# Two causal score products of a gated linear attention as 64-row matmul pairs, each head parity in a PSUM bank of its own

## The reference

```python
def step1(hk, inp):
    qi, ki, si, gi = inp
    hk = hk * gi[:, :, None, :] + ki[..., None] * si[:, :, None, :]
    return (hk, jnp.einsum('bhk,bhkm->bhm', qi, hk))
_, ok = jax.lax.scan(step1, hk0, (q, k, s_norm, g))
qv = jax.nn.softmax(ok, -1)
def step2(hv, inp):
    qvi, si, vi, gi = inp
    hv = hv * gi[..., None] + si[..., None] * vi[:, :, None, :]
    return (hv, jnp.einsum('bhm,bhmv->bhv', qvi, hv))
_, ov = jax.lax.scan(step2, hv0, (qv, s_norm, v, g))
```

## Time and profile before

| | us |
|---|---|
| median of 3 runs | 1521.48 (1519.7 to 1524.4) |
| time of the profiled execution | 1518.72 |
| span of its trace | 1516.6 |

### The profile page before, as it was taken

The page is one execution under the profiler, slowest core; times in us unless marked ns, Lnnn a source line. Parts: engine busy times, 40 slices in busy tenths (PEclk is TensorE's granted clock), DMA queues, the critical chain, the costliest instruction groups (busy, mean ns, idle before and its releaser), DMA issues.

```text
span 1516.6 us, 31405 instructions
## 1 busy us (share of the span) xinstructions
PE 1456.9 (96%) x10520; PEld 1291.4 (85%) x10520; DVE 1217.1 (80%) x3006; ACT 961.4 (63%) x2531; POOL 828.6 (55%) x937
## 2 busy tenths in 40 slices
PE   5798999999999999999999999999999999999975
PEld 3577989889889988988989888889988989989764
DVE  3668888888888888888888888888888888888642
ACT  3456666766666667666666766666667666666541
POOL 2355555656665565565556656655565565556420
PEclk9999999999999999999999999999999999999987
DMA  8230100011110001111100011110001111000000
GB/s 250 98 100 18 24 10 23 17 24 24 25 24 15 18 16 24 24 24 24 24 10 23 17 24 24 24 24 10 23 16 24 24 24 24 21 13 18 17 7 14
DMA packets 113102, 45.03 MB, mean 30 GB/s; under 512 B 86192, under 2 KB 109104, under 8 KB 112944
## 3 DMA queue, kind: packets, MB, share of 16 engines
q1 hardware_dynamic: 112944, 43.03, 11.3%
HBM read 26.74 MB, written 16.25 MB: 28 GB/s over the span
## 4 chain that ended last, share of the span: by engine, by line
PE 91%; DVE 3%; issue 2%; POOL 1%; ACT 1%; DMA 1%; SPq 0%; POOLq 0%; DVEq 0%; ACTq 0%
PE bank L444 76%; PE bank L450 7%; PE bank L685 5%; PE bank L770 2%; PE bank L532 1%; DVE a_conv L887 1%; PE bank L738 0%; DVE a_rC L909 0%; ACT x_prob L1331 0%; SPq L433 0%; DMA x_prob<-in_ctxT 0%; DVE x_nmax L1013 0%; DMA x<-in_x 0%; PE bank L541 0%; DVE x L1035 0%
## 5 line engine op out<-in xcount | busy, mean ns | idle before, releaser
L1331 ACT ACTIVATE x_prob<-bank,x_nmax 128x77 f32<-128x77 f32 x1024 | 248.5, 329 | 51.2 <-DVE x_nmax L1013 50.2
L1013 DVE TENSOR_REDUCE x_nmax<-bank 128x4 f32<-128x308 f32 x256 | 120.1, 469 | 109.8 <-PE bank L444 106.0
L1344 ACT ACTIVATE x_probT<-bank 128x256 f32<-128x256 f32 (+1 forms) x256 | 112.2, 438 | 98.3 <-PE bank L685 98.1
L1497 POOL TENSOR_TENSOR a_orinv<-a_ove,mhalf 128x8 f32<-128x8 f32 x32 | 65.1, 2035 | 199.1 <-DVE a_ove L952 199.1
L444 PE MATMUL bank<-x_Vbd,x_probT 128*128 128x34 f32 (+1 forms) x1280 | 162.5, 267 | 0.7 <-DVE x_o L1027 0.7
L887 DVE SCALAR_TENSOR_TENSOR a_conv<-a_raw,cw,a_conv 128x256 f32<-128x256 f32 x384 | 155.0, 478 | 7.5 <-POOL a_conv L1459 7.5
L444 PEld LDWEIGHTS bank<-x_Vbd,x_probT 128*128 128x128 f32 x1280 | 158.0, 192 | 1.1 <-DVE x_o L1027 1.1
L685 PE MATMUL bank<-ident,x_prob 128*128 128x128 f32 x640 | 114.6, 277 | 0.4 <-ACT x_prob L1331 0.3
L909 DVE RECIPROCAL a_rC<-bank 128x512 f32<-128x512 f32 x32 | 107.1, 3348 | 0.6 <-PE bank L444 0.6
L912 DVE TENSOR_TENSOR a_AT<-bank,tri 128x512 f32<-128x512 f32 x128 | 87.7, 685 | 23.9 <-PE bank L444 23.9
L444 PE MATMUL bank<-x_K_bd,x_Q_stack 128*128 128x308 f32 x256 | 94.5, 369 | 8.6 <-ACT x_prob L1331 5.2
(11 more groups left out here) (271 smaller groups left out, 5264.0 us busy)
## 6 DMA issues: line engine op xcount, KB each, us to landing
x<-in_x SPq DMA_DIRECT2D x32, 256.0 KB, 2.6
out<-x SPq DMA_DIRECT2D x32, 256.0 KB, 2.2
x_K_stack<-k_hi SPq DMA_DIRECT2D x64, 77.0 KB, 2.6
k_hi<-f_sT_hi SPq DMA_DIRECT2D x5, 512.0 KB, 2.8
k_lo<-f_sT_lo SPq DMA_DIRECT2D x5, 512.0 KB, 3.8
v_tok<-x_probT SPq DMA_DIRECT2D x10, 256.0 KB, 3.4
x_KT_lo<-k_lo SPq DMA_DIRECT2D x32, 77.0 KB, 2.3
x_Vbd<-v_tok SPq DMA_DIRECT2D x128, 9.6 KB
```

The costliest lines, as they stand in the source:

```text
L1013: dve.tensor_reduce(nmax[:, u % 2, :], X0[:, 0:UH * S2].rearrange("p (h s) -> p h s", h=UH), AX.X, ALU.min).then_inc(on.x_max, 1)
L1331: ins = act.activation(prob[:, col:col + S2], X0[:, i * S2:(i + 1) * S2], ACT.Exp, scale=-1.0, bias=nmax[:, u % 2, i:i + 1])
L1344: act.activation(probT[:, g[0]:g[-1] + 1, :].rearrange("p h t -> p (h t)"), X1[:, 0:len(g) * P], ACT.Copy).then_inc(on.x_pT, 1)
```

## The change

Both triangular products are cut along the contraction into rows 0 to 63 and rows 64 to 127, which hold two heads each. The upper half (`i = 0`) writes A0 in `a_A` and A1 in `a_P`, the lower half the other bank. `a_q_bd` shrinks to two column blocks (`h % 2`), so the A product has four matmuls of 64 rows by 256 columns in place of two of 128 by 512. `a_qn_bd` and `a_qn_last` give way to one dense `a_qnT`, copied in one ACT instruction, and the P product has eight matmuls of 64 by 128 in place of four of 128 by 256. A bank now holds both chunks of two heads, in place of one chunk of all four; `a_AT` is laid out the same way. In the order for PE, `a_A` is one step behind `x_turn`, and `a_P` is one step.

```diff
-        q_bd = [sb(f"a_q_bd_{i}", [P, H, T]) for i in range(2)]
+        q_bd = [sb(f"a_q_bd_{i}", [P, 2, T]) for i in range(2)]
...
-        AT = sb("a_AT", [P, TC, H, P])
+        AT = sb("a_AT", [P, 2, TC * 2, P])
...
-        qn_bd = sb("a_qn_bd", [P, 2, 2, T])
-        qn_last = sb("a_qn_last", [P, 2, P])
+        qnT = sb("a_qnT", [P, 2, T])
...
-            def a_A(r, c):
-
-                if c == 0:
-                    pe.wait_ge(on.a_qbd, upto(r))
-                    if r > 0:
-                        pe.wait_ge(on.a_oT, upto(r - 1))
-                        pe.wait_ge(on.a_oTl, upto(r - 1))
-                else:
-                    pe.wait_ge(on.a_ktok, upto(r))
-                mm((A0 if c == 0 else A1)[:, :], qkr[r % 2][:, 1, c * P:(c + 1) * P],
-                   q_bd[r % 2][:, :, c * P:(c + 1) * P]).then_inc(on.a_A_ps, 1)
+            def a_A(r):
+
+                pe.wait_ge(on.a_qbd, upto(r))
+                if r > 0:
+                    pe.wait_ge(on.a_oT, upto(r - 1))
+                    pe.wait_ge(on.a_oTl, upto(r - 1))
+                pe.wait_ge(on.a_ktok, upto(r))
+                for c in range(TC):
+                    for i in range(2):
+                        rows = slice(i * P // 2, (i + 1) * P // 2)
+                        ins = mm((A0 if i == 0 else A1)[:, c * D:(c + 1) * D], qkr[r % 2][rows, 1, c * P:(c + 1) * P],
+                                 q_bd[r % 2][rows, :, c * P:(c + 1) * P])
+                        if c == TC - 1:
+                            ins.then_inc(on.a_A_ps, 1)
...
-            def a_P(r, c):
-
-                pe.wait_ge(on.a_qnT, upto(r, 3))
-                dst = A1 if c == 0 else A0
-                for f in range(2):
-                    ins = mm(dst[:, f * 2 * P:(f + 1) * 2 * P], ET[r % 2][:, f, c * P:(c + 1) * P],
-                             qn_bd[:, f, :, c * P:(c + 1) * P])
-                ins.then_inc(on.a_P_ps, 1)
+            def a_P(r):
+
+                pe.wait_ge(on.a_qnT, upto(r))
+                for c in range(TC):
+                    for f in range(2):
+                        for i in range(2):
+                            rows = slice(i * P // 2, (i + 1) * P // 2)
+                            ins = mm((A1 if i == 0 else A0)[:, c * D + f * P:c * D + (f + 1) * P],
+                                     ET[r % 2][rows, f, c * P:(c + 1) * P], qnT[rows, f, c * P:(c + 1) * P])
+                            if c == TC - 1 and f == 1:
+                                ins.then_inc(on.a_P_ps, 1)
...
-                A(a_vtok); N(g_mm, 0); N(g_mm, 1); A(a_ktok); A(a_A, 0); X(x_turn); A(a_A, 1); A(a_state)
...
+                A(a_vtok); N(g_mm, 0); N(g_mm, 1); A(a_ktok); X(x_turn); A(a_A); A(a_state); N(g_mm, 2)
...
             def a_maskA(r, c):
-                dve.wait_ge(on.a_A_ps, upto(r, TC, c + 1))
+                dve.wait_ge(on.a_A_ps, upto(r, 2))
                 causal(AT[:, c], (A0 if c == 0 else A1)[:, :]).then_inc(on.a_A, 1)
...
             def a_maskP(r, c):
-                dve.wait_ge(on.a_P_ps, upto(r, TC, c + 1))
+                dve.wait_ge(on.a_P_ps, upto(r, 2))
                 causal(PT[:, c], (A1 if c == 0 else A0)[:, :]).then_inc(on.a_P, 1)
...
-                    ins = act.activation(q_bd[r % 2][s, h, :], qkr[r % 2][s, 0, :], ACT.Copy)
+                    ins = act.activation(q_bd[r % 2][s, h % 2, :], qkr[r % 2][s, 0, :], ACT.Copy)
...
             def a_qnt(r):
                 act.wait_ge(on.a_qnT_ps, upto(r))
-                src = A0[:, :].rearrange("p (f t) -> p f t", f=2)
-                for hh in range(2):
-                    s = slice(hh * M, (hh + 1) * M)
-                    act.activation(qn_bd[s, :, hh, :], src[s], ACT.Copy).then_inc(on.a_qnT, 1)
-                act.activation(qn_last[:], src[:, :, P:2 * P], ACT.Copy).then_inc(on.a_qnT, 1)
+                act.activation(flat(qnT), A0[:, :], ACT.Copy).then_inc(on.a_qnT, 1)
```

More of the change, by code:

```diff
@@ L575, in a_ok @@
                     out = A1[:, D + h * M:D + (h + 1) * M]
-                    ins = mm(out, AT[:, 1, h, :], e[:, 1, h * M:(h + 1) * M], start=False)
+                    ins = mm(out, AT[:, h // 2, 2 + h % 2, :], e[:, 1, h * M:(h + 1) * M], start=False)
                 ins.then_inc(on.a_ok_ps, 1)
@@ L599, in a_o @@
                     if h % 2 == 0:
-                        mm(A1[:, D + f * P:D + (f + 1) * P], qn_last[:, f, :], state[:, D + f * P:D + (f + 1) * P],
+                        mm(A1[:, D + f * P:D + (f + 1) * P], qnT[:, f, P:2 * P], state[:, D + f * P:D + (f + 1) * P],
                            stop=False)
                     out = A1[:, D + h * VD:D + (h + 1) * VD]
-                    ins = mm(out, PT[:, 1, h, :], v[:, 1, h * VD:(h + 1) * VD], start=False)
+                    ins = mm(out, PT[:, h % 2, 2 + h // 2, :], v[:, 1, h * VD:(h + 1) * VD], start=False)
                 ins.then_inc(on.a_o_ps, 1)
@@ L797, in F @@
                         f(rf, *k)
-                A(a_vtok); N(g_mm, 0); N(g_mm, 1); A(a_ktok); A(a_A, 0); X(x_turn); A(a_A, 1); A(a_state)
[L801 to L807, removed]
+                A(a_vtok); N(g_mm, 0); N(g_mm, 1); A(a_ktok); X(x_turn); A(a_A); A(a_state); N(g_mm, 2)
+                N(a_turn); X(x_q); F(f_turn); A(a_ok); N(a_qk); X(x_s, 0); F(f_gate); F(f_u0); N(g_mm, 3)
+                X(x_pt, 0); X(x_s, 1); F(f_lg); N(a_v); A(a_qt); X(x_s, 2); F(f_v0); N(a_s); X(x_s, 3); A(a_P)
+                X(x_pt, 1); X(x_av, 0); X(x_s, 4); X(x_pt, 2); A(a_o); X(x_av, 1); X(x_pt, 3); F(f_st, 0)
+                X(x_s, 5); N(g_mm, 4); N(a_g); F(f_u1); X(x_pt, 4); X(x_av, 2); X(x_s, 6); F(f_v1); X(x_pt, 5)
+                X(x_av, 3); N(g_mm, 5); X(x_s, 7); N(g_mm, 6); N(a_c); X(x_pt, 6); A(a_ot); N(g_mm, 7)
+                X(x_av, 4); F(f_st, 1); X(x_pt, 7); X(x_av, 5); X(x_av, 6); X(x_av, 7); N(a_et); A(a_wo)
+                X(x_ot); F(f_yy); X(x_proj)
             def others():
@@ L812, in others @@
                 pe.wait_ge(w_lo, ALL_SPLIT)
-                pe.wait_ge(z_ready, 4)
+                pe.wait_ge(z_ready, 3)
             pe.wait_ge(ld_w, W_LANDED)
@@ L1160, in others @@
                 split(other_splits, len(splits))
-                dve.wait_ge(z_ready, 4)
+                dve.wait_ge(z_ready, 3)
             dve.memset(mhalf[:], -0.5).then_inc(w_ready, 1)
@@ L1414, in others @@
                 split(other_splits)
-                act.wait_ge(z_ready, 4)
+                act.wait_ge(z_ready, 3)
             act.wait_ge(ld_w, W_LANDED)
@@ L1567, in others @@
                 pool.memset(prob[:], 0.0).then_inc(z_ready, 1)
-                pool.wait_ge(z_ready, 4)
+                pool.wait_ge(z_ready, 3)
             pool.wait_ge(ld_w, W_LANDED)
```

7 lines of the change are left out of this document (3 added, 4 removed).

## The result

| | us |
|---|---|
| before, median of 4 runs | 1521.1 (1519.7 to 1524.4) |
| changed kernel, median of 4 runs | 1542.7 (1540.1 to 1545.1) |
| ratio, 95% interval | 1.0138 (1.0111 to 1.0166) |
| span of the trace, before and after | 1516.6 and 1538.7 |

The change costs 21.6 us. The forecast was a cost of 35 us, 1556.5, with a range from 1537 to 1590.

A forecast was written before the change was run, and what follows sets the result against it. PE was taken as the bound, with matmuls in flight in 96% of the span. A + P - 1.46 gave +1.13 us a pass, +35 us over 31 passes on 1521.5: 1556.5 us, range 1537 to 1590.

The forecast's parts named there:

- steps 1 and 5: Start of a pass: PE empty before `x_turn`, 0.86 us; `a_state` waits for a whole mask, 1.02 behind the A product.
- step 3: A product: eight 256-column instructions, halves overlapping in five steps of 0.215, 1.07 us; 1.72 if not overlapped.
- step 4: Switch from 128 to 64 rows: between 0 and 0.10 us, taken as 0.10.
- the term that was mis-sized: P product: 1.73 us before, 1.42 after with 0.10 for the switch, a gain of 0.31 a pass.
- nine steps: P product's overlapped bound: sixteen 128-column matmuls in nine steps, 0.97 us, if the two halves' loads run side by side.
- step 6: Behind P: both masks start at its end, so `a_o` can start 1.64 behind it, a new wait of 0.21 us.
- the sum: Pass total: A + P - 1.46, +1.13 us; the start of the pass up to `a_state` makes +1.23 of it.
- The serial case: Rival: halves of A and P don't overlap, +2.19 us a pass, 1589; chance 0.17 including nearly serial.
- The case in which everything overlaps: Rival: A and P overlap, loads too, switches free; +0.58 us a pass, 1539.5; within the forecast's 0.75.
- The faster case: Rival: A and P passes at one-pass matmul pace, A + P below 1.46, -0.32 us a pass, 1511.5; chance 0.05.
- The granted clock: Sign that the forecast is wrong: PE's granted clock, 1.00 in a steady pass, falls with the new gaps.

The follow-up runs named there:

- The order alone: Kernel before with its full-row products, only PE's order changed: first A product moved behind `x_turn`; 1543.3 us, ratio 1.0155.
- the better order: Changed kernel with the keys turned first and the cut A product back in front of `x_turn`; 1510.6 us, ratio 0.9937.
- The swap on POOL: Kernel with only the P product cut, and on POOL the experts' product `f_sw(0)` put in front of the clip; 1507.6 us, ratio 0.9909.
- the halves of A apart: Changed kernel with the upper half of A in front of `x_turn` and the lower half behind it; 1524.0 us, ratio 1.0022.
- A's halves in turn: Changed kernel with loops turned in A and P, all products of the upper half before the lower half's; 1555.1 us, ratio 1.0239.

## Why the prediction was right, and where it was off

The sign, the places and the mechanism held; the size was 13 us too large. A pass was forecast 0.32 too long, and 0.24 of that, 7 us, is P. Another 2 us are the shorter tail, which the forecast didn't cover.

- **The two new waits** (steps 1 and 5) are as forecast: PE idle in front of `x_turn` (0.79 against 0.86, since `x_turn` now starts 0.06 behind the end of `x_out`, where behind the A product it started 0.12 behind it) and a whole mask in front of `a_state`. The order alone shows them with old products, and the better order takes them away.
- **The A product** (step 3) was put at 1.07 plus a switch and takes 0.97 behind the switch: its pairs start at 717.22, 717.54, 717.75 and 717.97, and the last takes 0.215. The mask starts 1.21 behind its start, where 1.07 + 0.20 was booked, and `a_state` 2.05 against 2.09. The figure came out near by luck, since its derivation was wrong. I had the lower half wait for the upper half's second pass, five steps. Instead all eight run in four pairs, 0.86, and the first pair takes 0.10 more, which I hadn't booked. The trace shows the first two of the pass at once, and four in flight soon after (first in the stretch 717.20 to 717.50, then in 717.50 to 717.70):

```profile
717.22 0.49 PE L443 MATMUL bank<-a_q_bd,a_qkr 64*128 64x256 f32 x2
```

```profile
717.22 0.70 PE L443 MATMUL bank<-a_q_bd,a_qkr 64*128 64x256 f32 x4
```

- **The switch** (step 4): 0.10 was booked before A and before P. `x_turn` to A takes 0.59 with it and 0.49 in the run with the old products in the same order, so 0.10; in front of P the stretch grew by 0.09. But that is a third of the price: 0.10 more lies in the first instruction behind it and 0.10 in the switch back to 128 rows, about 0.3 around a half of A standing alone.
- **The P product is the term that was mis-sized.** I took the middle, 1.42 with its switch, between loads one after the other (1.68) and loads side by side (0.97). It is 1.09 + 0.09 = 1.18, not far above the lower bound with its switch, 1.07: loads overlap. The lower bound was derived from nine steps; there are eight pairs, 0.86, and the price of the switches, so it is near for the same lucky reason as in A. (Of the bounds given for the gain, 0.76 leaves the switch out and the loss of 0.10 has it in.) A load of 64 rows takes 0.18 to 0.19 like one of 128. That is the rule of the Trainium skill, "TensorE: Matmul & The Clock Gate", section "LDWEIGHTS (loading the stationary operand)", that a load goes by its columns, and it was not what decided. "Different tiles can execute LdWeights and Matmul in parallel", in the Trainium skill, "TensorEngine Tiling (Array Packing)", section "Key Properties", was, and the runs bear it out with 0.97 against 1.52 for the same sixteen loads. The term is 0.24 a pass, 7 us.
- **The wait in front of `a_o`** (step 6) was put at 0.21 and is 0.06 from start to start: the first mask starts 0.14 behind P, where 0.20 was booked, and `a_o` 0.06 behind the second, where 0.15 was. Another 0.10 shows inside `a_o`: its first eight instructions take 0.94 from start to start where they took 0.84. All of it lies in the first, 0.16 where it was 0.06; that its load is no longer hidden behind other work is the likely reason, and not shown.
- **What I didn't book**: the transpose of o hangs on a chain over DVE and POOL that starts behind P's masks, and that chain grew by 0.18 a pass. The swap on POOL takes the longer convolution away and gives 0.08 back; I put the other 0.10 down to the slower start of `a_o`, which no run isolates. Against that, `a_turn` to `a_ok` gave 0.09 back: before, `x_q` started 0.15 behind the end of its operand `x_xnT_lo` and so waited for it; in the changed kernel it starts 0.43 behind.
- **What the sum hides**: it has the order and the cut of A in one figure, +1.23, with the mask behind the whole of A, which is right. But full-row products in the same order would have let the first mask go halfway, so that A's cut is itself a loss there, 0.23 of the measured 1.16.
- **The rivals.** The serial case (1589) is refuted. The case in which everything overlaps (1539.5) was nearest. The faster case needed A + P below 1.46; they are about 2.25. The granted clock, whose fall would have been a sign of being wrong, stayed at 1.00 in such a pass.

Per pass: +1.13 forecast, less 0.07 at the start, 0.24 in P, 0.05 in `a_o` and 0.09 before `a_ok`, plus 0.08 behind `a_o` and 0.06 elsewhere, are 0.82, the measured 0.81 but for rounding.

The best kernels of the study are those with P alone in halves and A as it was: 0.9930 of the kernel before, and 0.9909 with the swap on POOL, a difference that isn't clear of the noise.

## What to carry to other kernels

A product that may be halved in time is worth nothing in a place where it stood over somebody else's wait: look first what else the step was covering (here `x_out` and a mask), and measure the order apart from the arithmetic. Look also at when its reader may start: the full-row product let the first mask go halfway, the cut one only at its end. Two half-array products into two banks do overlap, loads too, so the place to use them is where PE itself sets the pace. Behind it look for the chain on the other engines that starts at the same point, since it keeps its own length.

## What the runs showed of the hardware

- Products on 64 rows, two row halves into two banks: eight passes of 256 columns in 1.14 us, four of them alone in 1.13.
- Around a group on 64 rows the switch costs about 0.3 us in all: 0.09 in front, 0.10 in its first instruction, 0.10 behind it (the halves of A apart).
- The order of writing made no difference to A: with four passes of one half written before four of the other, they still run in pairs, so later instructions of the other half start before earlier ones of the first. P, with eight of each, takes 1.64 in place of 1.09, and its first four stand alone. The Trainium skill, "TensorE: Matmul & The Clock Gate", section "The mechanism", has matmuls start and end strictly in program order; with A's halves in turn that can't be, as 1.14 us for the eight leaves no room for one half after the other at 1.06 each, and the first two start together. The measurement decides.
- A convolution step on DVE, which reads two tensors from SBUF, took 0.70 us in place of 0.48 when a POOL product ran 0.42 us into it; with 0.12 us of another POOL instruction it took 0.48. The Trainium skill, "GPSIMD Engine Reference", section "1. Specifications", says that the two contend when a DVE instruction has two SBUF inputs; the first of the two runs agrees, and the second shows no loss.
